# Query copies ahead of the exponentials, and another order of the side tasks in the first sixteen slots of a fused cross-attention and feed-forward kernel

## What is computed

```python
def attention(query, key, value, ...):            # 16 heads, dk = dv = 64
    q = einsum('bnd,hdk->bhnk', query, proj_q) + bias_q
    k = einsum('bnd,hdk->bhnk', key, proj_k) + bias_k
    v = einsum('bnd,hdv->bhnv', value, proj_v) + bias_v
    attn = softmax(einsum('bhqk,bhnk->bhqn', q, k) / 8)
    hid = heads side by side of einsum('bhqn,bhnv->bhqv', attn, v)
    return hid @ w_out.T

def ffn(x, w_gate, w_up, w_down):
    h = silu(fp4_linear(x, w_gate)) * fp4_linear(x, w_up)
    return fp4_linear(h, w_down)      # fp4_quant_dequant of both operands in blocks of 16

x = x + attention(layernorm(x), ctx, ctx, ...)    # x: 2 x 1024 x 256, ctx: 2 x 154 x 256
x = x + ffn(layernorm(x), w_gate, w_up, w_down)
```

## Time and profile before

| | |
|---|---|
| median of 3 runs | 424.98 us (424.27 to 427.12) |
| profiled execution | 426.62 us |
| its span | 424.8 us |
| PE busy | 342.5 us (81%) |
| DVE busy | 319.3 us (75%) |
| ACT busy | 262.0 us (62%) |
| POOL busy | 254.2 us (60%) |

### The profile page before, as it was taken

One profiled execution on the slowest core, in us unless ns is written; L12 is line 12 of the kernel. 1 busy time (PEld: TensorE's weight loads), 2 busy tenths in 40 slices (PEclk: granted clock), 3 DMA queues, 4 the chain that ended last, 5 costly groups with the idle time before them and its releaser, 6 DMA issues.

```text
span 424.8 us, 9531 instructions
## 1 busy us (share of the span) xinstructions
PE 342.5 (81%) x3595; PEld 257.3 (61%) x3595; DVE 319.3 (75%) x634; ACT 262.0 (62%) x635; POOL 254.2 (60%) x248
## 2 busy tenths in 40 slices
PE   1877567799898878988879777479778999999985
PEld 1554355577666666766667565356555777677764
DVE  2978445657876688767878985367999999999692
ACT  3655677777797887877878688532451535543331
POOL 6361233746768786678777757524783777686610
PEclk9989689999999999999999999689898999999999
DMA  7971335646768787797888678701100000000001
GB/s 220 322 287 31 64 62 80 128 88 104 129 133 152 139 128 135 132 141 138 130 154 138 132 104 159 142 2 30 35 0 15 12 26 12 26 14 13 27 25 39
DMA packets 125375, 40.86 MB, mean 96 GB/s; under 512 B 117452, under 2 KB 123280, under 8 KB 125329
## 3 DMA queue, kind: packets, MB, share of 16 engines
q1 hardware_dynamic: 125329, 40.25, 47.5%
HBM read 8.78 MB, written 2.10 MB: 26 GB/s over the span
## 4 chain that ended last, share of the span: by engine, by line
DVE 44%; ACT 20%; PE 19%; issue 10%; POOL 5%; DMA 1%; SPq 0%; ACTq 0%; DVEq 0%
ACT arena L831 10%; DVE negmax L1069 8%; PE ps L483 5%; PE ps L485 4%; PE ps L484 4%; DVE arena L1085 4%; DVE arena L1146 4%; DVE arena L1148 3%; DVE arena L1100 3%; DVE arena L1267 3%; DVE arena L1233 2%; POOL arena L1338 2%; ACT arena L841 2%; POOL arena L1343 2%; DVE arena L1104 2%
## 5 line engine op out<-in xcount | busy, mean ns | idle before, releaser
L1338 POOL TENSOR_TENSOR arena<-arena 128x640 f16<-128x640 f32 x64 | 89.6, 1400 | 87.2 <-ACT arena L841 86.8
L831 ACT ACTIVATE arena<-ps,negmax 128x154 f32<-128x154 f32 x256 | 78.8, 392 | 50.0 <-DVE negmax L1069 50.0
L562 PE MATMUL ps<-v_h,pT 128*128 128x132 f16 (+1 forms) x640 | 51.9, 211 | 13.2 <-DVE q_odd L1061 7.2
L1343 POOL TENSOR_TENSOR arena<-arena 128x256 f16<-128x256 f32 x64 | 50.5, 791 | 8.7 <-ACT arena L848 8.7
L562 PEld LDWEIGHTS ps<-v_h,pT 128*128 128x128 f16 x640 | 37.9, 98 | 22.2 <-issue 20.9
L1069 DVE TENSOR_REDUCE negmax<-ps 128x4 f32<-128x616 f32 x64 | 50.6, 791 | 0.3 <-PE ps L617 0.2
L483 PE MATMUL ps<-arena 128*128 128x256 f16 (+1 forms) x144 | 42.0, 292 | 8.4 <-DVE arena L974 6.0
L841 ACT ACTIVATE arena<-arena 128x640 f16<-128x640 f32 x64 | 48.5, 757 | 0.1
L483 PE MATMUL ps<-arena,xnT_even 128*128 128x352 f16 x128 | 41.0, 320 | 4.2 <-DVE xnT_even L1156 4.2
L484 PE MATMUL ps<-arena 128*128 128x256 f16 (+1 forms) x144 | 41.8, 290 | 0.0
L485 PE MATMUL ps<-arena 128*128 128x256 f16 (+1 forms) x144 | 41.8, 290 | 0.0
(11 more groups left out here) (155 smaller groups left out, 951.8 us busy)
## 6 DMA issues: line engine op xcount, KB each, us to landing
out_dram<-arena SPq DMA_DIRECT2D x16, 128.0 KB, 1.7
pT<-arena SPq DMA_TRANSPOSE x70, 4.0
xs<-in_x_dram SPq DMA_DIRECT2D x2, 512.0 KB, 7.2
arena<-in_L_xattn_w_out_dram SPq DMA_DIRECT2D x1, 1024.0 KB, 12.0
xs<-in_x_dram SPq DMA_DIRECT2D x2, 384.0 KB, 6.6
wffn<-in_L_ffn_w_down_dram SPq DMA_DIRECT2D x1, 704.0 KB, 9.6
wffn<-in_L_ffn_w_gate_dram SPq DMA_DIRECT2D x1, 640.0 KB, 7.6
wffn<-in_L_ffn_w_up_dram SPq DMA_DIRECT2D x1, 640.0 KB, 8.5
```

The lines of the kernel that those rows point to most:

```text
L562: last = pe.matmul(o[:, h0 * HB:h1 * HB], pT[:, n % RING_P, part * CHUNKS + c], v[:, b, j, at[0]:at[-1] + 1].rearrange("p m k -> p (m k)") ...
L831: last = act.activation(prob[:, j, k * LP:k * LP + L], ps[:, 2 * (j % 2) + k % 2, (k // 2) * L:(k // 2 + 1) * L], ACT.Exp, bias=negmax[:, ...
L1338: pool.tensor_tensor(part_of(j, 1), prob[:, j], part_of(j, 0), ALU.subtract).then_inc(p_low, 1)
L1343: pool.tensor_tensor(hid_part(n, 1), hidden_f[:, n % 2], hid_part(n, 0), ALU.subtract).then_inc(hid_low, 1)
```

## The change

It has three parts.

1. In each slot the query tasks come first in `tasks_of`, so PE multiplies them right behind the scores. ACT copies the high part of a query before the exponentials of the slot, where it did so after them. DVE still writes the low part of a query ahead of the next row maximum; the low parts of all other tasks (rows, values, output weights, scaled heads) now stand behind that maximum.
2. The rows of the second step are turned in slot 5 (were: 3), and its query tasks stand in slots 6 to 9 (were: 4 to 7). The layernorm that they need is cut over slots 1, 2 and 3 of DVE (were: 0, 1 and 2), and ACT waits for it in slot 4.
3. The output weights are turned in slots 4, 4, 5, 6 (were: 6, 8, 9, 10), and the values of the second batch are computed in slots 10 to 13 (were: 11 to 14).

```diff
         def values_at(b, n):
-            return n if b == 0 else 11 + n
+            return n if b == 0 else 10 + n
         def wot_at(n):
-            return (6, 8, 9, 10)[n]
+            return (4, 4, 5, 6)[n]
         def rows_at(i):
-            return 3 if i == 1 else 8 * (i - 1) - 1
+            return 5 if i == 1 else 8 * (i - 1) - 1
         def query_at(i, p):
-            return 4 + p // 2 if i == 1 else 8 * (i - 1) + 1 + p
+            return 6 + p // 2 if i == 1 else 8 * (i - 1) + 1 + p
...
         def tasks_of(n):
-            out = [("x", i) for i in range(1, STEPS) if rows_at(i) == n]
+            out = [t for i in range(1, STEPS) for t in query_tasks(i) if query_at(i, t[2]) == n]
+            out += [("x", i) for i in range(1, STEPS) if rows_at(i) == n]
             out += [t for t in VALUES if values_at(t[1], t[2]) == n]
             out += [t for t in WOUT if wot_at(t[1]) == n]
-            out += [t for i in range(1, STEPS) for t in query_tasks(i) if query_at(i, t[2]) == n]
...
@@ ACT, slot(n)
+                for t in tasks_of(n):
+                    if t[0] == "q": high(t)
                 exps(n)
                 for t in tasks_of(n):
-                    high(t)
-                if n == 2: act.wait_ge(ln_step, 2 * LN_STEPS)
+                    if t[0] != "q": high(t)
+                if n == 4: act.wait_ge(ln_step, 2 * LN_STEPS)
...
@@ DVE, slot(n)
                 if n >= 1:
                     for t in tasks_of(n - 1):
-                        low(t)
+                        if t[0] == "q": low(t)
                 row_max(n)
+                if n >= 1:
+                    for t in tasks_of(n - 1):
+                        if t[0] != "q": low(t)
...
@@ DVE, first(n)
+                if n == 1:
                     dve.wait_ge(stats_done, 2 * STEPS)
                     layernorm(1, STEPS, LN_STEPS, [0, 1])
-                if n == 1: layernorm(1, STEPS, LN_STEPS, [2, 3])
-                if n == 2: layernorm(1, STEPS, LN_STEPS, [4])
+                if n == 2: layernorm(1, STEPS, LN_STEPS, [2, 3])
+                if n == 3: layernorm(1, STEPS, LN_STEPS, [4])
```

## The result

The changed kernel takes 408.69 us, the median of 4 runs (407.15 to 410.05), beside 425.7 for the kernel before on the same chip: a ratio of 0.960 [0.9547, 0.9652]. The forecast was 410, with a range of 401 to 418. The profiled execution took 407.99 us, with a span of 406.1, so the two spans differ by 424.8 - 406.1 = 18.7 us.

The account below looks back on a forecast made before the run. An ACT-DVE chain was taken to bound each slot, no engine being full. Savings of 6.0 (start), 7.0 (middle), 1.3 (slots 48 to 55) and 0.5 (end) sum to 14.8 us, giving 410 for the median, range 401 to 418.

Parts of the forecast that it names:

- The chain and the plain slot: Ordinary slot: ACT and DVE taking turns set 3.18 us; with that chain gone, PE's row of work sets 2.65.
- The slots that aren't ordinary: Middle steps of eight slots (m is the slot in the step): 25.4 us against 27.15, four steps saving 7.0.
- The one in front of m=0: Gap of 3.64 us: after rows are turned, the heads of m=7 wait for the scaling, now behind the maximum.
- The one in front of m=7: Gap of 2.71 us: the maximum comes late behind the second half of the weight grid on DVE.
- the case that half of the grid halves are short: Middle step: 24.9 us instead of 25.5 where half of the grid halves find POOL idle.
- the grid on DVE: Weight grid in m=5 and m=6: both halves together between 1.8 and 4.5 us, taken as 3.8.
- The first sixteen slots: Start-up: slot 10 comes 9.2 us earlier, then values' low parts give some back in slots 11 to 14; 6.0 saved.
- The aside on the weights: Start-up slots: turning the output weights, four of 0.5 us on PE, only changes place.
- The end: Last seven slots, without queries: only the maximum goes ahead of the scaling, which waited for POOL; 0.5 us saved.
- That the banks don't bite: Rival for the middle steps: a step falls to ACT's work, about 23.3 us; 402 in all, chance 0.12.
- That only the start is gained: Rival: bank waits and POOL's lateness eat the middle's gain, steps stay at 27; 418 us, chance 0.17.
- POOL, at 81.2 of 99.6 us, never came to be the bound: Rival: slots wait for POOL, then query, copy and exponentials, 3.6 us a slot; slower, 432 us, chance 0.04.

Follow-up runs that it names:

- the last two kernels above: Rows behind the heads plus low parts placed slot by slot, against the changed kernel, with the residual sum ahead of or behind the scaling: 399.24 and 401.39 us.
- The order alone: Only part 1 of the change (task order within a slot), on the kernel before, with side tasks in their old slots: 415.09 us, ratio 0.9763.
- the places alone: Only parts 2 and 3 of the change (new slots for the side tasks), on the kernel before: 425.67 us, ratio 0.9991.
- values and weights first: Changed kernel with rows behind the heads, and low parts of values and output weights again ahead of the row maximum: 408.94 us, ratio 0.9602.
- the successor: Changed kernel with rows behind the heads, low parts placed by slot, and the residual sum of m=2 ahead of the scaling: 399.24 us, ratio 0.937.
- the rows last: Changed kernel with the rows task behind the heads in its slot on every engine, nothing else: 405.38 us, ratio 0.954.

## Why the prediction was right, point by point

**The chain and the plain slot.** Forecast 2.65, measured 2.65, and the kernel with the copy behind the exponentials shows both links by themselves. The chain was read whole from one slot, start to start.

**The slots that aren't ordinary.** The gaps behind the exponentials of m=7, 0, ... 6, in us, after the change:

| gap in front of | m=0 | 1 | 2 | 3 | 4 | 5 | 6 | 7 |
|---|---|---|---|---|---|---|---|---|
| predicted | 3.64 | 3.65 | 2.74 | 3.51 | 2.65 | 3.14 | 3.44 | 2.71 |
| measured | 3.42 | 3.64 | 2.65 | 3.50 | 2.65 | 3.05 | 3.36 | 2.62 |

Six of the eight gaps have the cause that the working gave them. The one in front of m=0 has it in part (below). The one in front of m=7 has another: the working had DVE late behind the grid, and in slots 30 and 31 ACT works from the exponentials at 143.70 to those at 146.32 without a wait. The sum is 24.9 where I took 25.4, so four steps gave 9.0 us, not 7.0, and with the early start slot 56 came at 225.67 us, not 229; the working had named 24.9 for the case that half of the grid halves are short. Half of the 0.6 us between the eight gaps and the working lies in front of m=0 and m=7, where the working had DVE late behind the grid; the other half are 0.09 us each in front of m=2, 5 and 6, estimates of ACT's and DVE's rows. The term that was mis-sized is the grid on DVE, which I took at 3.8 us for both halves. They take 0.88 each in most cases:

```profile
L1167 DVE SCALAR_TENSOR_TENSOR arena<-arena x6: 880/881/1141, 87.7 to 215.6; 128x704 f32<-128x704 f32 x6
```

```profile
L1170 DVE SCALAR_TENSOR_TENSOR arena<-arena x6: 879/881/1181, 93.6 to 219.1; 128x704 f32<-128x704 f32 x6
```

That is 1.76 for both, just under the 1.8 that I gave as the lower bound, against 2053 + 1802 ns in the earlier trace rows. It saves DVE 2.1 us a step, or 8.4 in the middle stage, and this is nearly all of the fall of its busy time by 9.6. Most of it lay beside ACT's work, which sets the gaps in front of m=6 and 7 anyhow. And part came back at m=7, by POOL. Its low part of the probabilities there took longer, and the low part of the heads came behind it (slots 30 and 31):

```profile
143.08 0.88 DVE L1170 SCALAR_TENSOR_TENSOR arena<-arena 128x704 f32<-128x704 f32 x1
...
143.28 1.94 POOL L1344 TENSOR_TENSOR arena<-arena 128x640 f16<-128x640 f32 x1 [0.65 <-ACT arena L841]
...
145.18 0.67 POOL L1349 TENSOR_TENSOR arena<-arena 128x256 f16<-128x256 f32 x1
```

The scaling waits for this L1349 and starts at 145.96. With POOL's usual 1.40 it would have started some 0.5 earlier; that is worked out and not tried. So the wait of the heads at m=7 has the length I forecast, 1.21 us, and another cause at its far end.

**The first sixteen slots.** Forecast 6.0, measured 5.4. The dates came near what was worked: exponentials of slot 10 at 69.97 (70.3) and of slot 16 at 99.95 (about 101), from a start of slot 0 that was itself 1.65 earlier. Measured from slot 0, slot 10 took 37.39 us (36.1 forecast) and the six slots behind it 29.98 (30.5 forecast). So the date of slot 10 is right by luck: the early start and the longer way to it cancel. The sizes inside differ. Slots 4 and 5 came 0.3 us earlier from slot 0 than I had carried them (12.37 and 16.03), and slot 6 took 7.57 where I had 5.9. Its queries waited for the low rows:

```profile
48.17 1.12 PE L590 MATMUL ps<-ident,arena 128*128 128x128 f32 x4 [3.93 <-ACT arena L862]
...
53.94 0.27 PE L483 MATMUL ps<-xnT_odd,wq_h 128*128 128x256 f16 x1 [1.59 <-DVE xnT_odd L1125]
...
55.45 0.84 ACT L796 ACTIVATE q_odd<-ps,biasT 128x256 f16<-128x256 f32 x2 [3.02 <-PE ps L485]
56.18 1.23 ACT L831 ACTIVATE arena<-ps,negmax 128x154 f32<-128x154 f32 x4
```

These rows answer to the earlier trace rows. The stall of ACT (3.02 us) is the mechanism that I had named for this slot, and the 5.9 held it. What the working lacked fits the clock, which was 0.50 from 46.0 to 52.8 us: the last two kernels above, one program up to slot 17, have 5.88 us in this slot with 0.95 from 49 to 54 us, and 8.12 with 0.50. That the gain is given back in slots 11 to 14 held as well: gaps of 4.81, 5.79, 6.31, 5.98, 3.72 and 3.37 from slot 10 on, forecast 4.6, 5.8, 6.3, 6.0, 3.9 and 3.9. That these waits are the values' low part behind the maximum is shown by the kernels that put it ahead. The aside on the weights didn't hold (above). It had no price of its own in the sum, since the gaps had been worked with the tasks in their slots.

**The end.** The last seven gaps gave 0.6 (forecast 0.5), but by another sum. The order alone, with the same order there, has 21.69 us in this stage and the change 22.95. The difference is in slot 59:

```profile
233.56 0.27 PE L578 MATMUL ps<-wot_h,pT 128*128 128x256 f16 x1 [0.90 <-DVE xs L1093]
...
234.89 0.34 PE L617 MATMUL ps<-kT_l,q_odd 64*128 64x154 f16 x2
...
236.61 1.23 ACT L831 ACTIVATE arena<-ps,negmax 128x154 f32<-128x154 f32 x4 [2.16 <-DVE negmax L1071]
```

PE had waited 0.90 us for the residual sum, and from 234.0 to 237.0 us it ran at a granted clock of 0.50, the level of 1.2 GHz, with score matmuls of 0.34 instead of 0.23 us. Against the 21.69 of the order alone, the stage would have gained 1.8 us. That the forecast of 0.5 met the measured 0.6 is luck.

**What wasn't forecast.** 1.65 us of the span come from ahead of slot 0. The change moves nothing there, and over the profiles of this study slot 0 begins between 32.4 and 34.8. The clock divides them. The window from 20 to 32 us, the kernel before and then the changed one:

```profile
20.00:32.00 12.00, 9.29 (x73) 6.77 (x70) 9.46 (x21) 7.33 (x15) 7.99 (x4) 0.86 0.80 287
```

```profile
20.00:32.00 12.00, 7.71 (x73) 6.00 (x71) 10.23 (x25) 6.99 (x15) 7.04 (x4) 1.00 0.82 291
```

In the five profiles with 0.86 there (both of the kernel before, the first of the places alone, the copy behind the exponentials, and values and weights first) slot 0 begins at 33.83 to 34.75; in the nine with 1.00 it begins at 32.37 to 33.23. The places alone have one profile of each kind, so it isn't the kernel that decides. Without the 1.65 the two spans differ by 17.1 us; the medians differ by 425.7 - 408.69 = 17.0.

**The rivals.** That the banks don't bite was wrong for this kernel (7.5 us of heads waiting for the scaling) and its step came nearly true in the successor (23.9 us), though some waits for banks are left there. That only the start is gained fell with the middle's 9.0. POOL, at 81.2 of 99.6 us, never came to be the bound; DVE's scaling waits for it for 5.2 us in all.

## What to carry to other kernels

When two engines take turns in every slot, write the chain start to start, move the one link that can go elsewhere, and then compute for each kind of slot which resource is next; here that gave eight gaps within 0.22 us. The places were worth nothing in medians alone and 6.4 us with the order on, so test such a change in both halves and each half on top of the other. And where tasks take banks in turn, ask of every instruction that empties a bank in which slots the next task takes that bank, and put it ahead of the slot's own work in those, which is a choice by slot, not by class. Here that and the rows last were worth another 9.4 us in medians, 6.1 of them beyond the rows last alone. A difference of some 2 us between two single profiles is to be read beside the granted clock, window by window.

## What the runs showed of the hardware

**Who starts first holds the SBUF.** I had expected that a denser POOL would lengthen DVE's grid halves. The reverse happened. The first half and POOL beside it in slot 29, before the change:

```profile
149.79 1.40 POOL L1338 TENSOR_TENSOR arena<-arena 128x640 f16<-128x640 f32 x1 [1.83 <-ACT arena L841]
149.88 2.05 DVE L1165 SCALAR_TENSOR_TENSOR arena<-arena 128x704 f32<-128x704 f32 x1
```

The same two after it:

```profile
139.86 0.88 DVE L1167 SCALAR_TENSOR_TENSOR arena<-arena 128x704 f32<-128x704 f32 x1
139.89 2.11 POOL L1344 TENSOR_TENSOR arena<-arena 128x640 f16<-128x640 f32 x1 [1.16 <-ACT arena L841]
```

Before, POOL starts 0.09 us ahead, takes its 1.40, and DVE's half takes 2.05. After, DVE starts 0.03 us ahead, takes its 0.88, and POOL takes 2.11. Over all 64 the operation on POOL has a minimum, median and maximum of 1391, 1399 and 2112 ns after, and 1394, 1399 and 1422 before, while the halves on DVE went from 2053 and 1802 to 881. So the side that pays is the one that starts second, here by 0.09 and 0.03 us. In all kernels with the query's copy ahead of the exponentials the price fell on POOL for at least the first half (means on DVE of 954 to 1029 ns); in all with the copy behind them it fell on DVE (1806 to 1883). The kernel with the copy behind differs from the changed one by ACT's order alone, and there POOL starts 0.09 us ahead again and DVE's half takes 2.06. For POOL as a whole little changed: before, its low part of the heads started 1.27 us behind that half and took 1.31, where its median is 0.67. Now it pays in the other of its two low parts: they kept it busy for 89.6 + 50.5 us before and 94.7 + 44.2 after, so POOL in all pays no more than it did, and what DVE saved is a gain. In both pictures the later one ends 2.14 us behind the start of the earlier, near the 1.40 + 0.88 = 2.28 of one behind the other. The Trainium skill ("SBUF — State Buffer", "Who interferes with whom") has this: the two exclude each other for a whole instruction, and "Issue order, not op shape, decides who blocks." The trace agrees with both sentences. I had used the first and not the second. ACT's L841 releases POOL's operation and starts at 148.96 before and 139.05 after; POOL follows it by 0.83 and 0.84, DVE's half by 0.92 and 0.81. The change, which takes DVE's wait for the query's copy out of the way of the maximum, moved the half ahead by 0.11 us, and so past POOL's start.

**The clock of a short stall.** Up to slot 16 some of these kernels are the same program, and still differ by some 2 us. In the profile of the chosen places the gap of slot 6 is 5.88 us, and 8.12 in the kernel that differs from it only in the residual sum from slot 18 on. From 49 to 54 us the two had granted clocks of 0.95 and 0.50, with PE busy for under half of the 5 us ahead in both. Of the 9.4 us by which the better kernel wins, its profile owes some 2 to this (the changed kernel has 7.57 in that slot); the kernel without the residual's new place, which had the slow start in its profile, still wins by 7.3 in medians.
